# A post-norm attention and mixture-of-experts kernel: the mask's product opens the score bank, and three pieces of VectorE work stand later

## What is computed

```python
Q, K, V = sign(x * sign(bv_q)), sign(x * sign(bv_k)), x * sign(bv_v)
scores = einsum('btd,bsd->bts', Q, K) / 16
attn = where(causal, sigmoid(4 * scores), 0)
x = layernorm(x + attn @ V)
# then a mixture of experts with 32 experts, one per row:
# router logits, softmax, argmax, at most 320 rows per expert
# out = silu(row @ w_gate[e]) * (row @ w_up[e]) @ w_down[e], times the gate
x = layernorm(x + out)
```

## Time and profile before

| | |
|---|---|
| median of three runs | 545.31 us |
| the profiled execution, its own time | 545.93 us |
| its span, first to last instruction | 543.1 us |
| TensorE busy (share of the span) | 516.6 us (95%) |
| VectorE busy | 404.9 us (75%) |
| ScalarE busy | 378.9 us (70%) |
| GpSimd busy | 377.4 us (69%) |

### The profile page before, as it was taken

How to read it: one execution, slowest core, us unless ns; L and a number is a source line. 1 busy time by engine, 2 the same in 40 slices (tenths; PEclk the granted TensorE clock), 3 DMA queues, 4 the chain that set the end, 5 groups by cost and what they waited for, 6 DMA issues and landing times.

```text
span 543.1 us, 12159 instructions
## 1 busy us (share of the span) xinstructions
PE 516.6 (95%) x3990; PEld 458.2 (84%) x4028; DVE 404.9 (75%) x1026; ACT 378.9 (70%) x775; POOL 377.4 (69%) x497
## 2 busy tenths in 40 slices
PE   6999999999999999999999989999999999999992
PEld 5889888888888898888888837999998899999981
DVE  3775787885767957878856735888888888888873
ACT  5885968768867869687686523667776767777752
POOL 4646877776878678777777171477677777787776
PEclk9999999999999999999999999999999999999997
DMA  8995332263232253338761016377777666776211
GB/s 252 362 351 183 94 98 61 78 175 100 98 89 84 90 115 100 94 49 263 172 234 56 7 37 163 90 230 216 213 226 221 196 196 200 211 242 194 75 41 49
DMA packets 91902, 81.52 MB, mean 150 GB/s; under 512 B 31626, under 2 KB 83066, under 8 KB 91840
## 3 DMA queue, kind: packets, MB, share of 16 engines
q1 hardware_dynamic: 84848, 66.39, 42.5%
q0 software_dynamic: 6912, 14.30, 7.6%
q10 hardware_dynamic: 80, 0.07, 0.0%
HBM read 44.33 MB, written 37.90 MB: 151 GB/s over the span
## 4 chain that ended last, share of the span: by engine, by line
PE 87%; issue 4%; DVE 3%; POOL 3%; ACT 1%; DMA 1%; ACTq 0%; DVEq 0%; POOLq 0%; SPq 0%
PE ps L918 12%; PE ps L919 11%; PE ps L920 11%; PE ps L894 10%; PE ps L1074 8%; PE ps L1082 7%; PE ps L1075 7%; PE ps L1100 5%; PE ps L1108 3%; PE ps L1047 3%; PE ps L937 2%; PE ps L950 2%; PE ps L1097 1%; PE ps L1099 1%; PE ps L1098 1%
## 5 line engine op out<-in xcount | busy, mean ns | idle before, releaser
L918 PE MATMUL ps<-v_hl,hl_ring 128*128 128x256 f32 x544 | 176.0, 324 | 0.5 <-DVE hl_ring L1170 0.3
L919 PE MATMUL ps<-v_hl,hl_ring 128*128 128x256 f32 x544 | 153.4, 282 | 0.0
L920 PE MATMUL ps<-v_hl,hl_ring 128*128 128x256 f32 x544 | 153.1, 282 | 0.0
L918 PEld LDWEIGHTS ps<-v_hl,hl_ring 128*128 128x128 f32 x544 | 103.3, 190 | 15.9 <-issue 1.4
L1170 DVE TENSOR_TENSOR hl_ring<-ps,hl_ring 128x512 fp32r<-128x512 f32 (+3 forms) x160 | 93.4, 602 | 23.2 <-ACT ps L695 17.4
L919 PEld LDWEIGHTS ps<-v_hl,hl_ring 128*128 128x128 f32 x544 | 103.6, 190 | 2.4
L920 PEld LDWEIGHTS ps<-v_hl,hl_ring 128*128 128x128 f32 x544 | 103.2, 190 | 0.0
L693 ACT ACTIVATE hl_ring<-ps 128x512 fp32r<-128x512 f32 (+3 forms) x160 | 85.8, 536 | 23.1 <-PE ps L894 10.9
L695 ACT ACTIVATE ps<-ps 128x512 f32<-128x512 f32 (+3 forms) x160 | 87.1, 544 | 0.0
L535 POOL DMA_INDIRECT expert_rows<-xrow,slot x64 | 64.5, 1008 | 29.2 <-issue 24.9
L894 PE MATMUL ps<-q_t,k_t 128*128 128x512 bf16 (+3 forms) x285 | 77.7, 346 | 5.9 <-issue 2.4
(11 more groups left out here) (163 smaller groups left out, 1104.9 us busy)
## 6 DMA issues: line engine op xcount, KB each, us to landing
expert_rows<-xs SPq DMA_DIRECT2D x40, 258.0 KB, 6.0
xs<-expert_rows SPq DMA_DIRECT2D x32, 258.0 KB, 2.8
xall<-in_L_attn_x_dram SPq DMA_DIRECT2D x16, 512.0 KB, 5.3
out_dram<-alone SPq DMA_DIRECT2D x16, 512.0 KB
xall<-in_L_ffn_w_gate_dram SPq DMA_DIRECT2D x32, 256.0 KB
xall<-in_L_ffn_w_up_dram SPq DMA_DIRECT2D x32, 256.0 KB
xall<-in_L_ffn_w_down_dram SPq DMA_DIRECT2D x32, 256.0 KB
xs<-expert_rows SPq DMA_DIRECT2D x31, 64.5 KB
```

What stands on the lines that cost most here:

```text
L918: mm(o, ah, v_hl[:, 0, j, :], start=(j == 0 and i % 2 == 0), stop=False, skip_group_check=True)
L919: mm(o, ah, v_hl[:, 1, j, :], start=False, stop=False, skip_group_check=True)
L920: last = mm(o, al, v_hl[:, 0, j, :], start=False, stop=(j == GT * g + i), skip_group_check=True)
```

## The change

On a diagonal step the mask's product comes first and opens the bank (`start=True`), and the two score products add to it; the last of them now closes it. Outside the mask's 128 columns the first score product writes, as nothing stands there since the bank was opened. On VectorE the row statistics of tiles 0 and 1 get a table of their own, `ROWS`: for group 0 they stand behind step 5 in place of 4, for group 3 behind step 41 in place of 40 (step 1 of the next batch), for groups 1 and 2 where they were. The second `residual` of group 3 moves from step 40 to 41. The two key instructions of group 3 move from step 24 to steps 26 and 27.

```diff
-SUM = {0: (4, 4), 1: (13, 13), 2: (23, 24), 3: (40, 40)}
+SUM = {0: (4, 4), 1: (13, 13), 2: (23, 24), 3: (40, 41)}
+ROWS = {0: 5, 1: 13, 2: 24, 3: 41}
-KEY = {1: (1, 3), 2: (8, 10), 3: (24, 24), 0: (31, 33)}
+KEY = {1: (1, 3), 2: (8, 10), 3: (26, 27), 0: (31, 33)}
...
                 diag = j >= GT * g
+                if diag:
+
+                    mm(ps[:, k % SB, lo:lo + P], identb[:, :], maskb[:, :], start=True, stop=False,
+                       skip_group_check=True)
                 for c in range(DC):
                     last = mm(o, k_t[:, c, j * P:(j + 1) * P], q_t[:, g, c, lo:GQ],
-                              start=(c == 0), stop=(c == DC - 1 and not diag))
-                if diag:
-                    last = mm(ps[:, k % SB, lo:lo + P], identb[:, :], maskb[:, :], start=False, stop=True)
+                              start=(c == 0 and not diag), stop=(c == DC - 1), skip_group_check=diag)
                 last.then_inc(scores_ready, 1)
...
             def add_pair(b, g, i):
                 residual(b * NG + g, i, b * NS + END[g] - GT + i + 2, g % 2)
-                if i > 0:
-                    row_statistics(b * NG + g, i - 2, g % 2)
...
+                        if k == ROWS[g]:
+                            row_statistics(b * NG + g, 0, g % 2)
+                        if k + NS == ROWS[g] and not first:
+                            row_statistics((b - 1) * NG + g, 0, g % 2)
```

## The result

The changed kernel takes 539.0 us (median of 6 runs, 538.01 to 540.19) against 544.97 us for the kernel before in the same session (6 runs, 543.85 to 545.62). The ratio is 0.9892, with a 95% interval from 0.9882 to 0.9903: 1.1% faster, some 5.9 us. The forecast was 542.5 us, with a range from 540.3 to 545.3.

What follows compares the result with a forecast made beforehand. TensorE was taken to bound the attention, its gain arriving at the end one to one. Terms 2.4 + 1.0 + 1.2 - 0.5 - 0.9 - 0.2 = 3.0 us gave a forecast of 542.5 us, range 540.3 to 545.3.

Steps and rivals of the forecast that it cites:

- The masks: Diagonal steps: with the mask's product first, 0.05 us of idling saved on 3 of 4 steps, 2.4 us.
- The keys: Step 25: moving group 3's keys to 26 and 27 cuts TensorE's idling by 0.24 us, 1.0 us in all.
- Group 0's row statistics: Step 5: with the statistics moved behind it, TensorE no longer idles 0.30 us for `low`; four times, 1.2 us.
- What a seam gives back: Three seams between batches: TensorE arrives 0.3 us early but VectorE's chain does not, so 0.9 us is lost.
- Group 3 between batches: Seams: `low` 41 waits for ScalarE, delaying the second residual; -0.45, +0.4 and -0.45 us, a loss of 0.5 us.
- The allowance: Attention: 0.2 us taken off the gain for small waits that come last once TensorE is earlier.
- the order works everywhere: Seams: if `low` 40 is not late, nothing is given back and waits go; 5.2 us gained, 540.4 us; 17%.
- The slower rival: `values` of step 40: TensorE waits for the second residual, 3.2 us lost at the seams; 546.0 us; 12%.
- long GpSimd instruction: Moved keys fall beside a GpSimd multiplication, making `low` 28 1.5 us later; 1.8 us gained, 543.8 us; 7%.

Runs made afterwards that it cites:

- e1: The kernel before with only the mask's product moved first on diagonal steps; 542.86 us, ratio 0.9961.
- e8: The kernel before, unchanged, profiled once more in another execution; 543.96 us in this one run.
- e7: The changed kernel, but with group 3's second residual and row statistics left at step 40; 540.54 us, ratio 0.9905 to the kernel before.
- e9: The changed kernel plus one extra ScalarE copy to scratch ahead of the weights of steps 40, 80 and 120; 540.77 us, ratio 0.9932 to the kernel before.

## Why the prediction was right or wrong

- **The masks, 2.4 us: right.** 0.05 us on three of four diagonal steps and none on the step of 128 columns. The gap did not move to the front: mask to next product is 0.06 us. In e1 alone some 0.4 us of it went back at steps 5 and 25; with those waits gone all of it arrived. The estimate from the Trainium skill, "TensorE: Matmul & The Clock Gate", section "Back-to-back issue gap" (81 ns, which made 1.4 us), is too small here: the trace shows 0.06 us for this pair, and the measurement decides.
- **The keys, 1.0 us: right, a little low.** 0.24 to 0.44 us at step 25, 1.1 us against the first trace and 1.3 against e8, and their new place costs nothing.
- **Group 0's row statistics, 1.2 us: right.** 0.27 us at step 5, four times: 1.1 us.
- **"What a seam gives back", -0.9 us: wrong.** TensorE does arrive 0.33 us earlier (the lead falls from 2.55 to 2.22), but the seam stays at 5.62 us in e1 and e7. The step failed where it said that VectorE's chain "hangs on ScalarE": in the old order the chain that holds TensorE starts at TensorE's own last product, through the second residual. It moves with TensorE.
- **"Group 3 between batches", -0.5 us: wrong, in its premise.** Measured: +0.38 us at each seam, 1.15 together. The mechanism is as I wrote it, wait and all, and e9 shows it at work, at 0.25 us a seam where I had put 0.45. But it needs the late `low` 40, and I read that off a single execution in which VectorE had lost 1.39 us at step 33. I took VectorE's idling of 2.45 us ahead of `low` 40 for the sign of lateness. It is none: in e8 VectorE idles 2.33 us there, with `low` 40 starting 1.39 us earlier, and in the changed kernel 2.42. The lead would have told. The 0.74 us of idling that I counted on at the second seam was in part that execution's as well, 0.5 us of it.
- **The allowance, -0.2 us:** in e1 such waits took some 0.4 us back; in the changed kernel no row answers to it.

With the failed steps replaced: 2.4 + 1.3 + 1.1 + 1.15 = 5.95 us, against 542.2 - 536.3 = 5.9 us between the spans of e8 and the changed kernel. Against the trace I predicted from, another 0.5 us of its second seam are in the difference, and 0.3 us by which the two executions start apart (the first load for `values` at 12.43 and 12.12 us).

Of the rivals, "the order works everywhere" came true, in its condition (`low` 40 is not late) and in its mechanism. Its 5.2 us fall 0.7 short: they count only the waits of 0.2 us a seam, while the seam wins 0.38, and the keys won up to 0.3 us more. My argument against it, that it was late in all three seams, was no argument about the kernel: three seams of one execution are not three executions. In none of the other eleven traces of this study is the lead below 2.1 us, but for the two kernels that were delayed on purpose. Why that one execution had `low` 40 late three times, once behind a pause of ScalarE and twice behind one of VectorE, stays open. The slower rival needed the same lateness, and even with it in place (e9) the kernel is faster than before. No key met a long GpSimd instruction at its new place.

## What to carry to other kernels

A short product should not stand right ahead of float32r weights: on 48 steps here that cost 0.05 us each, and both orders tried that ended on a longer product took it back. When a gain or a loss hangs on who is late at one place, ask what chain makes it late and read that place in a second execution before pricing it; here a pause of 1.39 us at step 33 gave the term of a place seven steps later the wrong sign. How long an engine idled there does not say whether it was late; the distance to the instruction that waits for it does. And follow a wait to its start before you say that it swallows a gain: a chain that starts at the bounding engine moves along with it.

## What was not expected of the hardware

Two executions of one program differed by pauses on VectorE and ScalarE, several in a batch. Such are 1.39 us on VectorE behind a product that started at the same time in both, 1.4 us (1.64 against 0.23) on ScalarE, and 0.5 us on VectorE at the second seam. They left little mark on the time: they shortened the lead of `low` 40 by 1.1 us, two of the three seams kept their 5.6 us, and the attention took 0.4 us more than in e8. At the reduction behind the logits' product, eleven of twelve traces show no such pause. What causes them, no run here shows.
